# Four-layer attention chain on one core: values by pairs of sequences, context on 64x32 tiles, a causal mask from 32-row tiles, folded text weights, and a new order

## The reference

```python
# layer 0: 16 heads of 8, causal (key < query), first query row set to zero; LN, relu FFN, LN
scores = where(j < i, q @ k.T / sqrt(8), -1e30); attn = softmax(scores); attn[:, :, 0, :] = 0
x = LN(x + (attn @ v) @ Wo + bo); x = LN(x + relu(x @ W1 + b1) @ W2 + b2)
# layer 1: 16 heads of 8, no mask, gelu FFN, no norms
x = x + (softmax(q @ k.T / sqrt(8)) @ v) @ Wo + bo; x = x + gelu(x @ W1 + b1) @ W2 + b2
# layer 2: text = x @ Wt.T + bt; vision = mean(ctx) @ Wv.T + bv (one row per sequence)
agreement = sum(text * vision, -1)
route = softmax(2 * agreement, over tokens)
gate = sigmoid(text @ Wg_t.T + (route * vision) @ Wg_v.T + bg)
x = LN(x + gate * route * vision) * gamma + beta
# layer 3: RMS norm, 16 heads of 64, x + softmax(q @ k.T) @ v @ wo
```

## Time and profile before

| | us |
|---|---|
| median of 3 runs (1565.29 to 1566.65) | 1566.12 |
| the profiled execution | 1565.23 |
| its span, first to last instruction | 1563.7 |
| busy on PE (matmuls) | 1464.4 |
| busy on DVE / ACT / POOL | 1066.7 / 994.1 / 490.9 |

### The profile page before, as it was taken

One profiled execution on the slowest core, in us unless ns is written; L12 is line 12 of the kernel. 1 busy time (PEld: TensorE's weight loads), 2 busy tenths in 40 slices (PEclk: granted clock), 3 DMA queues, 4 the chain that ended last, 5 costly groups with the idle time before them and its releaser, 6 DMA issues.

```text
span 1563.7 us, 48922 instructions
## 1 busy us (share of the span) xinstructions
PE 1464.4 (94%) x20384; PEld 1061.4 (68%) x20384; DVE 1066.7 (68%) x2490; ACT 994.1 (64%) x1893; POOL 490.9 (31%) x522
## 2 busy tenths in 40 slices
PE   5779999999999999999999999999999999999976
PEld 3446776767677676767767676776767677676755
DVE  4447868677776867778686776867677676767633
ACT  3236757667676766767676676757667575675754
POOL 3131423315142342514233251332325133142402
PEclk7769999999999999999999999999999999999999
DMA  4000000000000000000000000000000000000000
GB/s 138 14 1 15 3 9 16 9 15 3 21 3 8 16 9 14 3 21 3 8 16 9 15 3 21 3 9 15 9 14 3 17 8 9 1 3 8 3 7 9
DMA packets 27798, 20.02 MB, mean 13 GB/s; under 512 B 1088, under 2 KB 27200, under 8 KB 27328
## 3 DMA queue, kind: packets, MB, share of 16 engines
q1 hardware_dynamic: 27584, 16.90, 3.6%
HBM read 12.70 MB, written 4.19 MB: 11 GB/s over the span
## 4 chain that ended last, share of the span: by engine, by line
PE 83%; ACT 5%; DVE 5%; POOL 3%; issue 3%; DMA 0%; SPq 0%; ACTq 0%; DVEq 0%
PE bank L458 69%; PE bank L467 13%; POOL prob L870 2%; ACT probT L741 2%; ACT prob L809 2%; DVE negmax L944 1%; DVE sums L1084 1%; ACT Q L822 1%; POOL prob L850 1%; DMA Q<-in_split_weights 0%; DVE rinv L1088 0%; DVE sums L949 0%; DVE negmax L1078 0%; ACT prob L734 0%; DVE z L997 0%
## 5 line engine op out<-in xcount | busy, mean ns | idle before, releaser
L850 POOL TENSOR_TENSOR prob<-prob,rinv 128x512 f32<-128x512 f32 x256 | 262.1, 1043 | 333.2 <-DVE rinv L951 331.5
L734 ACT ACTIVATE prob<-bank 128x512 f32<-128x512 f32 x256 | 148.3, 601 | 139.2 <-PE bank L458 137.6
L467 PE MATMUL bank<-cst,prob 128*128 128x128 f32 x1536 | 212.4, 279 | 23.3 <-POOL prob L870 16.0
L870 POOL TENSOR_TENSOR prob<-prob,rinv 128x512 f32<-128x512 f32 x128 | 132.0, 1042 | 315.8 <-DVE rinv L1088 315.7
L467 PEld LDWEIGHTS bank<-cst,prob 128*128 128x128 f32 x1536 | 180.3, 143 | 69.1 <-issue 52.5
L944 DVE TENSOR_REDUCE negmax<-bank 128x8 bf16<-128x512 f32 x256 | 160.5, 670 | 68.4 <-PE bank L458 68.4
L949 DVE TENSOR_REDUCE sums<-prob 128x8 f32<-128x512 f32 x256 | 169.0, 660 | 12.6 <-ACT prob L734 10.3
L741 ACT ACTIVATE probT<-bank 128x512 f32<-128x512 f32 x256 | 144.6, 599 | 46.6 <-PE bank L467 46.6
L458 PE MATMUL bank<-negmax,ident_b 128*128 128x512 bf16 x384 | 134.8, 390 | 17.5 <-DVE negmax L944 10.1
L458 PE MATMUL bank<-room,wt 128*128 128x512 f32 x288 | 138.8, 592 | 0.0
L458 PEld LDWEIGHTS bank<-wt,Q 128*128 128x128 f32 x1024 | 122.8, 192 | 7.2 <-ACT Q L822 2.0
(11 more groups left out here) (137 smaller groups left out, 3081.9 us busy)
## 6 DMA issues: line engine op xcount, KB each, us to landing
x_in<-in_x SPq DMA_DIRECT2D x16, 256.0 KB, 2.9
c_in<-in_ctx SPq DMA_DIRECT2D x16, 256.0 KB, 3.3
out<-y SPq DMA_DIRECT2D x16, 256.0 KB, 2.3
Q<-in_split_weights SPq DMA_DIRECT2D x1, 1536.0 KB, 9.0
wt<-in_weights SPq DMA_DIRECT2D x1, 1024.0 KB, 10.0
wt<-in_weights SPq DMA_DIRECT2D x1, 640.0 KB, 5.9
wt<-in_weights SPq DMA_DIRECT2D x4, 128.0 KB, 9.7
cst<-in_constants SPq DMA_DIRECT2D x1, 229.0 KB, 2.5
```

The source lines that it names most:

```text
L467: last = nc.tensor.transpose(o[:, k * P:(k + 1) * P], src(k), ident)
L734: nc.scalar.activation(prob[l][:, t].rearrange("p c k -> p (c k)"), bank("S", l, u, t)[:, :], ACT.Exp, scale=SCALE8).then_inc(exp_ready.se ...
L850: nc.gpsimd.tensor_tensor(pr, pr, ri, ALU.mult).then_inc(norm_ready.sem, 1)
L870: nc.gpsimd.tensor_tensor(pr, pr, ri, ALU.mult).then_inc(norm3_ready.sem, 1)
```

## The change

- `v` has two steps of 4 sequences instead of four steps of 2. A pair of sequences stands in the weights (64 tokens each), not one sequence twice. `c_high` and `c_low` lose their doubled copies (512 instead of 1024 columns).
- `vm` makes two masked copies of each value; `O` is 32 products per step on tiles of 64 rows (one sequence of a pair, r) by 32 columns, in two banks; `ctx` is four DVE operations on 128 columns instead of two on 256.
- The mask is 16 bf16 products per `S` step, each 32 rows by 64 columns, 256 columns moving.
- `tp` and `tpT` go. Once, ahead of the first `q`, the text weights are multiplied into the gate's (`w_gate`, with `bt` into `bg_half`) and transposed (`w_text`). `gp` takes x directly; `gv` gets a second product of 8 columns, and `agree` multiplies x by its result.
- The order is now a sort: each step has a time of its own within a group (`PLAN`), each group a start (`START`). All four lists and all banks are placed anew.

```diff
-        k3.1@2 PT.1.1.0@2 PT3.3.1@3 PT.1.1.1@2 PT.1.1.2@2 PT.1.1.3@2 O3.3@3 O.1.1@2 v.3@1 k3.2@2 o.1@2
+        xT@0 cT@1.01 q.0@7.77 k.0@9.09 S.0.0@14.64 shift.0.0.0@17.91 shift.0.0.3@22.49 shift.0.0.2@22.71
...
+    placed = [(START[g] + at - AHEAD.get((kind, g), 0.0), kind, index, g) for g in range(G) for kind, index, at in plan]
+    return [step[1:] for step in sorted(placed, key=lambda step: step[0])]
...
-                    mm(bank("gv")[:, 0:GB], w("WgvT"), vis[:, cg, :]).then_inc(gv_filled.sem, 1)
+                    mm(bank("gv")[:, 0:GB], w("WgvT"), vis[:, cg, :])
+                    mm(bank("gv")[:, GB:2 * GB], w_text[:, :], vis[:, cg, :], start=False).then_inc(gv_filled.sem, 1)
...
-                        b = 2 * j + i
-                        twice = [part[:, cg, b].rearrange("p i k -> p (i k)") for part in (c_high, c_low)]
-                        last = split_mm(o[:, 2 * P * i:2 * P * (i + 1)], twice,
+                        pair = slice((2 * u + i) * P, (2 * u + i + 1) * P)
+                        last = split_mm(o[:, 2 * P * i:2 * P * (i + 1)], [part[:, pair] for part in context],
...
-                        for t in range(QUAD):
-                            mm(bank("S", l, u, t)[:, :], ident_b[:, :],
-                               causal_b[:, :].unsqueeze(1).broadcast_to([P, 8, L]), stop=False)
+                        for n in range(2):
+                            for t in range(QUAD):
+                                rows = slice(32 * t, 32 * t + 32)
+                                for a in range(2):
+                                    o = bank("S", l, u, t)[64 * a:64 * a + 64, :].rearrange("p (b k) -> p b k", k=L)
+                                    mm(o[:, :, 32 * n:32 * n + 32], causal_pick[rows, n, :],
+                                       causal_rows[rows, :].unsqueeze(1).broadcast_to([32, 8, 32]),
+                                       start=(n == 0), stop=False)
...
-                    for s in range(QUAD):
-                        for t in range(QUAD):
-                            cols = slice(32 * t, 32 * t + 32)
-                            last = mm(o[cols, s * P:(s + 1) * P], Vm[:, l, QUAD * u + s, cols],
-                                      probT[:, t, s, :], start=(s == 0))
+                    for j in range(2):
+                        for k in range(2):
+                            for r in range(2):
+                                rows = slice(64 * r, 64 * r + 64)
+                                for t in range(QUAD):
+                                    cols = slice(32 * t, 32 * t + 32)
+                                    last = mm(bank("O", l, u, r)[cols, j * P:(j + 1) * P],
+                                              Vm[rows, l, 2 * u + j, k, cols], probT[rows, t, 2 * j + k, :],
+                                              start=(j == 0 and k == 0))
...
-                elif kind == "tp":
+                elif kind == "gp":
                     pe.wait_ge(*ffn_ready(g, 1))
-                    mm(bank("tp")[:, :], w("WtT"), x1T[1][:, :]).then_inc(tp_filled.sem, 1)
-                elif kind == "gp":
-                    pe.wait_ge(*tpT_ready(g))
-                    mm(bank("gp")[:, :], w("WgtT"), tpT).then_inc(gp_filled.sem, 1)
+                    mm(bank("gp")[:, :], w_gate[:, :], x1T[1][:, :]).then_inc(gp_filled.sem, 1)
...
+            def text_weights():
+
+                pe.wait_ge(squares_loaded, 16)
+                nc.tensor.transpose(text_bank[:, 0:P], w("WtT"), ident).then_inc(text_filled, 1)
+                pe.wait_ge(text_ready, 1)
+                mm(text_bank[:, P:2 * P], w_text[:, :], w("WgtT"))
+                mm(text_bank[:, 2 * P:2 * P + 1], w("WgtT"), v("bt"), start=False).then_inc(text_filled, 1)
+                pe.wait_ge(text_ready, 2)
...
+                    for r in range(2):
+                        o = bank("O", l, u, r)[:, 0:2 * P].rearrange("p (j a q) -> p a j q", j=2, a=2)
+                        dve.wait_ge(*ctx_filled(g, l, u, part=r))
+                        nc.vector.tensor_scalar(half_ctx[:, r, :, q0:L], o[:, 0, :, q0:L], c("m_a", 0), v(f"bv{l}"),
+                                                ALU.mult, ALU.add).then_inc(half_ready.sem, 1)
```

More of the change, by code:

```diff
@@ L117, in parse @@
     kind, *index = name.split(".")
-    return kind, tuple(int(i) for i in index), int(at)
+    return kind, tuple(int(i) for i in index), float(at)
 def program(engine):
-    turn = [parse(token) for token in ORDER[engine].split()]
-    turns = G + max(at for name in ORDER for _, _, at in map(parse, ORDER[name].split()))
-    return [(kind, index, k - at) for k in range(turns) for kind, index, at in turn if 0 <= k - at < G]
-PROGRAM = {engine: program(engine) for engine in ORDER}
+    plan = [parse(token) for token in PLAN[engine].split()]
+    placed = [(START[g] + at - AHEAD.get((kind, g), 0.0), kind, index, g) for g in range(G) for kind, index, at in plan]
+    return [step[1:] for step in sorted(placed, key=lambda step: step[0])]
+PROGRAM = {engine: program(engine) for engine in PLAN}
 class Signal:
@@ L321, in xattn_sequence_kernel @@
         gelu_ready = Signal(sem("gelu_ready"), "ACT", "gelu", FT)
-        tpT_ready = Signal(sem("tpT_ready"), "ACT", "tpT")
         route_exp = Signal(sem("route_exp"), "ACT", "route")
@@ L473, in step @@
                 cg = g % 2
-                context = (c_high[:, cg, :, 0, :], c_low[:, cg, :, 0, :])
+                context = (c_high[:, cg, :], c_low[:, cg, :])
                 if kind == "xT":
@@ L537, in step @@
                             for a in range(2):
-                                last = mm(bank("S", l, u, t)[64 * a:64 * a + 64, s * P:(s + 1) * P],
-                                          Qm[l][rows, b, a, :], Km[l][rows, b].rearrange("p c k -> p (c k)"),
-                                          start=(l == 1 and s == 0))
+                                last = mm(blocks[t][64 * a:64 * a + 64, s // 2, :, s % 2, :], Qm[l][rows, b, a, :],
+                                          Km[l][rows, b], start=(l == 1 and s == 0))
                             if s == QUAD - 1:
@@ L614, in step @@
                     pe.wait_ge(*c_low_ready(g))
-                    first = b // 2 * 2 * P + L
-                    two = [part[:, cg].rearrange("p b i k -> p (b i k)")[:, first:first + P] for part in (c_high, c_low)]
-                    split_mm(bank("v3", b)[:, :], two,
+                    pair = slice(b // 2 * P, b // 2 * P + P)
+                    split_mm(bank("v3", b)[:, :], [part[:, pair] for part in context],
                              w_split("wv3", b % 2 * TOK, TOK)).then_inc(v3_filled.sem, 1)
@@ L878, in _ @@
             dve.tensor_copy(ident_b[:, :], ident)
-            dve.tensor_copy(causal_b[:, :], c("causal", 0, L))
+            dve.tensor_scalar(first_row[:, :], c("causal", L - 1), -1.0, -1e30, ALU.mult, ALU.add)\
+                .then_inc(first_row_ready, 1)
+            for t in range(QUAD):
+                rows = slice(32 * t, 32 * t + 32)
+                one = cst[rows, 32 * t:32 * t + 32]
+                dve.tensor_copy(causal_pick[rows, 0, 0:32], one)
+                dve.tensor_scalar(causal_pick[rows, 0, 32:L], one, 0.0, None, ALU.mult)
+                dve.tensor_copy(causal_pick[rows, 1, 0:32], one[:, 0:1].broadcast_to([32, 32]))
+                dve.tensor_copy(causal_pick[rows, 1, 32:L], one)
+            for r in range(2):
+                rows = slice(64 * r, 64 * r + 64)
+                own = cst[rows, CCOL["m_v"]:CCOL["m_v"] + P]
+                dve.tensor_copy(m_vc[rows, r, :], own)
+                dve.tensor_scalar(m_vc[rows, 1 - r, :], own, -1.0, 1.0, ALU.mult, ALU.add)
+            dve.wait_ge(first_row_ready, 1)
+            for t in range(QUAD):
+                rows, at = slice(32 * t, 32 * t + 32), CCOL["causal"] + 32 * (t % 2)
+                dve.tensor_scalar(causal_rows[rows, :], cst[rows, at:at + 32], first_row[rows, 0:1], None, ALU.min)
             nc.vector.tensor_tensor(m_c2[:, :], c("m_c", 0, 2), c("m_c", 2, 2), ALU.add)
@@ L1027, in step @@
                     dve.wait_ge(*gate_a(g))
[L1028 removed]
+                    nc.vector.tensor_tensor(gate_in, bank("gp")[:, :], agree_in, ALU.add).then_inc(gate_b.sem, 1)
                 elif kind == "vis_route":
```

215 lines of the change are left out of this document (124 added, 91 removed), and 30 rows, old and new, of the table BANK.

## The result

The changed kernel takes **1547.34 us** (median of 4 runs, 1543.82 to 1549.64) against 1566.38 for the kernel before, measured beside it: a ratio of 0.9874, 95% interval 0.9855 to 0.9894. It is faster, as forecast, but by 19 us and not by 43. The time lies inside the range (1504 to 1548), at its very edge.

What follows compares the result with a forecast made beforehand. PE's list of work was taken to set 13 turns of 91.80 us; -3.19 us work and +0.4 for order gave -2.8 a turn, -36.4. With beginning -2 and end -4, 1565.2 became 1522.8: predicted 1523 us, range 1504 to 1548.

Steps and rivals of the forecast that it cites:

- What bounds the kernel: Whole run: PE, busy 94% of the span and 97.99 of 100 us in the middle, sets the time.
- a turn lasts as long as PE's list of work: 13 equal group periods of 91.80 us: PE work removed shortens each; with +0.4 us for order, -2.8 us each.
- Context, +0.44 a turn: Four `O` steps per group, each 1.12 us with 64 instructions instead of 1.01 with 32: +0.44 us.
- Mask and text weights: Per group on PE: mask steps 0.29 us instead of 0.96, -1.34; `tp` gone, -0.85; second `gv` product, +0.20.
- the rival that they stand in a row: Mask steps: 16 weight loads in sequence cost 0.85 us a step, total 1541 us; chance 4%.
- The sum of work: PE's work per group: values -1.64, mask -1.34, `tp` -0.85, `gv` +0.20, context +0.44, together -3.19 us.
- the end: After group 15's input transposes: saved `tp`, values and mask against four dearer `O`, about -4 us.
- The beginning: Up to group 2's input transposes: +2.5 us for added early operations, about 4.5 given back, together -2 us.
- The new wait ahead of `out3.3`: Layer 3 output: `Q3` copies need 1.33 us, cover is 1.18, so 0.15 us new wait plus ACT's queue.
- the new order waits more: Rival: new step sequence in eight banks adds 1.5 us a turn beyond the charge, 1545 us; chance 16%.
- The slower case: Rival: `O` on 64x32 tiles keeps 31.6 ns an instruction, 2.02 us a step, 1581 us; chance 5%.
- a busy share under 96 in the middle: Sign of a wrong prediction: PE's middle busy share below 96, where 97.5 in 100 or a bit less was expected.

Runs made afterwards that it cites:

- a_vold: Changed kernel with its order, mask and folded weights, but values by four steps and 32-product contexts as before; 1536.72 us, ratio 0.9802.
- b_maskfold: Kernel before with only the new mask and folded text weights, in the old order with old values and contexts; 1546.06 us, ratio 0.9864.
- the moved `v3.6`: Third-layer value step placed between `S.0.1` and `O.0.0` in a_two; 0.91 us alone there, 0.69 in a row of its kind.
- b_split4: Kernel before with each context product of the first two layers issued as four of 32 columns; 1700.08 us, ratio 1.0852.
- c_mask8: a_vold with the mask by 8 products of 128 weight columns instead of 16; 1541.19 us, ratio 0.9834.
- a_two: Changed kernel with two moves alone, `v3.6` with `V3.6`, and `shift3.3.1`; 1552.75 us, ratio 0.9923.
- c_spread: a_vold with five PE steps moved apart (`v3.6` with `V3.6`, `v.0`, `q.1`, `shift3.3.1`, `PT3.1.0`); 1573.40 us, ratio 1.0042.
- b_wide: Kernel before with every 512-column product issued as two of 256; 1572.42 us, ratio 1.0032.

## Why the prediction missed, point by point

**What bounds the kernel:** right. PE's list sets the turn in every kernel here, and what came off it came off the time, but for what PE gave back by standing.

**The step that failed** is "a turn lasts as long as PE's list of work", with +0.4 us a turn charged for everything else. Work on PE fell by 89.41 - 86.76 = 2.65 us a turn. Idle time for other engines went from 2.00 to 1.94, so the 0.4 charged for the new order was not needed. But 1.86 - 0.23 = **1.63 us a turn** came in as stops put down to issue, a cost that no term of the sum held: -2.65 + 1.63 - 0.06 = -1.08. Of the 1.63 us, 1.38 are at the border, where PE waits for its instructions, and 0.25 are the short stops of the new order. The forecast for a turn was -2.79. The 1.71 us between the two are 1.63 of these gaps and 0.54 of work that did not come off, less the 0.46 by which the other waits stayed under their charge. Over 13 turns the gaps make 21 us, the missing work 7, and the overcharged waits give 6 back; the end adds 4 (below). The whole miss is 24 us by the median and 26 by the profiled execution. The earlier trace rows showed PE busy 97.99 in 100, and I took that as room without a limit of its own; the count of instructions per time was read nowhere, though each row shows it ("x32" against "x64").

**Context, +0.44 a turn:** the price of a step was right (1.08 for 1.12), the price of the choice was not. Per turn, values by pairs and contexts on 64x32 tiles take 87.62 - 86.76 = 0.86 us of work off PE (a_vold against the changed kernel) and bring 1.86 - 0.82 = 1.04 us of gaps (1.25 more at the border, 0.21 less elsewhere). In whole runs this part of the change loses 10 us. I forecast it as a gain of 1.64 - 0.44 = 1.20 us a turn.

**Mask and text weights:** the mask's own price came out better than forecast (0.24 for 0.29), and 16 loads of 64 columns passed in those 0.24 us and not in 0.85, so the rival that they stand in a row is out. In the old order (b_maskfold) mask and fold took 1.70 us of busy time off a turn where the terms said 1.99, and the 12 added mask products a step show in the gaps too (0.23 to 0.85).

**The sum of work,** -3.19 forecast and -2.65 measured: the steps' own prices would even give -1.44 (mask) - 1.52 (values) + 0.28 (contexts) - 0.85 (`tp`) + 0.23 (`gv`) = -3.30. The missing 0.65 is in no single step. Between steps of different kinds PE can lose time, as the moved `v3.6` shows; whether that is where it went stays open.

**The beginning,** -2: measured -2.2. `k.0` starts at 15.24 (15.5 forecast). **The end,** -4: measured +0.2, yet a_vold has 224.5 us there. After its last transposes of the inputs the changed kernel stands 8.4 us for issue, a_vold 4.0 and the kernel before 2.0 (7.7, 3.2 and 2.0 of it at the border). So the 4 us were gained and given back in the same way.

**The new wait ahead of `out3.3`** came as forecast at the end (the timeline's 1541.11 has 1.26 us for ACT's `Q`, as before) and cost nothing in the turns.

**The rivals:** the time is that of "the new order waits more" (1545), and for the wrong reason: other engines keep PE waiting no longer than before, and the short stops of the new order are 0.25 us a turn where the rival had 1.5. The slower case decided at an `O` of 1.78 us; it is 1.08. What I had named as the sign of a wrong prediction, a busy share under 96 in the middle, did show: the ten turns give 867.61 / 905.63 = 95.8%.

## What to carry to other kernels

Where products are of some 17 ns, count instructions as well as time: about 125 products in a row with their weight loads can stop TensorE for 0.3 to 1.8 us at a packet's border, as these runs have it, and a variant with half as many products of twice the rows can win although its work is longer. Read the waits put down to "issue" by kernel before and after any change that splits instructions, and look at whether they cut steps in the middle, and at places that drift from turn to turn. Keep steps of one kind together unless the gap that a separation closes is dearer than the 0.2 us that it costs.

## What the hardware showed unexpectedly

- Stops at the borders of instruction packets: one packet is 16.4 KB, and pairs of stops stand 125 products and as many loads apart. From one restart to the next were 3.60 us (541.87 to 545.47), 4.07 (1357.61 to 1361.68), and 3.83 in b_split4. These are not the shortest: over the 13 traces stops at neighbouring borders restart 2.95 (c_mask8) to 4.34 us (a_two) apart, and no two packets of PE's queue start less than 3.23 us apart (c_spread; 3.29 in the changed kernel). I take it, as an estimate from these, that PE is given no more than a packet in some 3.2 us. When a packet is asked for, and what takes this long, was not tried.
- Products added where each is long cost hardly any gaps (1504 in b_wide, +1.6 us); 2048 added where they take 17 ns cost 12.7 us.
- Halving a 128-column product on 128x32 tiles costs 0.1 us for 32 more products (work +6.1 us over 64 steps); quartering it lets the pitch rise from 17 to 21 ns.
- 16 mask products with 64 columns of weights take 0.24 us, 8 with 128 columns 0.33.
- The best version found is a_vold, 1537 us, 0.980 of the kernel before.
